# Second experts' rows scattered into token order, with TensorE weighing two of three blocks in the last stage

## The reference, cut to what matters

```python
y = layernorm(x)
topk_vals, topk_idx = top_k(y @ gate_w + gate_b, 2)
topk_w = softmax(topk_vals)
h = relu(y @ w1[e] + b1[e]);  expert_out = h @ w2[e] + b2[e]      # for the two chosen e
z = y + sum_k topk_w[k] * expert_out[topk_idx[k]]
out = x + (z - mean(z)) / sqrt(var(z) + 1e-5) * gamma + beta
```

## Time and profile before

| what | us |
|---|---|
| median of three runs | 5655.62 |
| profiled execution, own time | 5677.49 |
| its span in the trace | 5676.2 |
| experts' loop in its steady part | 5336 to 5586 |
| last stage, from its first instruction | 5594.9 to 5676.2 |

### The profile page before, as it was taken

The page is one execution under the profiler, slowest core; times in us unless marked ns, Lnnn a source line. Parts: engine busy times, 40 slices in busy tenths (PEclk is TensorE's granted clock), DMA queues, the critical chain, the costliest instruction groups (busy, mean ns, idle before and its releaser), DMA issues.

```text
span 5676.2 us, 62271 instructions
## 1 busy us (share of the span) xinstructions
PE 4234.6 (75%) x17066; PEld 2584.4 (46%) x17066; DVE 2738.1 (48%) x6256; ACT 1789.4 (32%) x4055; POOL 2420.1 (43%) x2811
## 2 busy tenths in 40 slices
PE   1111034457999999999999779487777776998798
PEld 0011012223544544545545338376666664665574
DVE  7998012222374254353222222665555557777535
ACT  4333000000100100101000221476666666998221
POOL 3788777774000000000000101677777775887124
PEclk9999567779999999999999889698888998999797
DMA  8900134456332222222322324577778774777423
GB/s 347 373 1 1 35 114 139 139 185 227 102 108 89 99 102 85 106 102 77 120 100 70 119 91 137 166 241 238 244 234 244 236 235 144 241 241 242 161 65 116
DMA packets 382809, 868.12 MB, mean 153 GB/s; under 512 B 87554, under 2 KB 187789, under 8 KB 355218
## 3 DMA queue, kind: packets, MB, share of 16 engines
q1 hardware_dynamic: 252002, 689.14, 34.7%
q0 software_dynamic: 76816, 147.75, 9.9%
q10 hardware_dynamic: 53664, 27.26, 1.7%
HBM read 579.84 MB, written 284.11 MB: 152 GB/s over the span
## 4 chain that ended last, share of the span: by engine, by line
PE 51%; POOL 26%; issue 10%; DVE 7%; DMA 5%; ACT 1%; DVEq 0%; SPq 0%; POOLq 0%; ACTq 0%
PE PS L1118 20%; POOL adjacency_more L581 10%; POOL mem L2043 9%; PE PS L2459 7%; POOL adjacency L581 7%; PE PS L1143 3%; PE PS L1145 3%; DMA mem<-gat_rows,mem 3%; PE PS L2879 2%; PE PS L1691 2%; PE PS L2899 2%; PE PS L1529 2%; PE PS L1148 2%; PE PS L1151 2%; PE PS L2086 1%
## 5 line engine op out<-in xcount | busy, mean ns | idle before, releaser
L1118 PE MATMUL PS<-mem 128*128 128x512 f32 (+1 forms) x3500 | 1400.8, 561 | 465.1 <-DVE mem L1260 461.1
L1118 PEld LDWEIGHTS PS<-mem 128*128 128x128 f32 x3500 | 639.3, 197 | 1187.3 <-issue 709.5
L2043 POOL DMA_INDIRECT mem<-gat_rows,mem x832 | 814.7, 979 | 261.2 <-issue 234.6
L1306 POOL TENSOR_TENSOR mem<-mem 128x256 f32<-128x256 f32 x25 | 20.2, 842 | 1784.1 <-DMA mem<-x 1784.1
L581 POOL DMA_INDIRECT adjacency_more<-mem x526 | 559.2, 1063 | 171.7 <-issue 171.7
L1191 ACT ACTIVATE mem<-PS 128x512 f32<-128x512 f32 (+1 forms) x35 | 19.0, 544 | 1706.8 <-PE PS L1118 1706.8
L2086 PE MATMUL PS<-mem 128*128 128x256 bf16 x2496 | 384.4, 294 | 118.2 <-issue 104.5
L2459 PE MATMUL PS<-mem 128*128 128x264 f32 x1660 | 462.8, 407 | 6.5 <-ACT mem L2447 2.4
L2124 ACT ACTIVATE mem<-PS,mem 128x256 f32<-128x256 f32 x832 | 424.0, 560 | 29.5 <-DVE mem L2151 15.7
L581 POOL DMA_INDIRECT adjacency<-mem x256 | 370.5, 1447 | 96.0 <-issue 80.6
L262 PE MATMUL PS<-mem 106*128 106x106 f32 (+4 forms) x446 | 93.7, 360 | 423.6 <-DVE mem L393 303.5
(11 more groups left out here) (437 smaller groups left out, 6931.1 us busy)
## 6 DMA issues: line engine op xcount, KB each, us to landing
mem<-adjacency SPq DMA_DIRECT2D x150, 1280.0 KB, 5.4
gathered_rows<-mem SPq DMA_DIRECT2D x416, 264.0 KB
mem<-gathered_rows SPq DMA_DIRECT2D x208, 528.0 KB, 4.5
adjacency<-mem SPq DMA_DIRECT2D x56, 800.0 KB, 20.7
adjacency_more<-mem SPq DMA_DIRECT2D x56, 800.0 KB, 21.5
mem<-adjacency_more SPq DMA_DIRECT2D x30, 1280.0 KB, 13.7
adjacency<-mem SPq DMA_DIRECT2D x30, 1280.0 KB, 11.1
mem<-edge_slots ACTq DMA_DIRECT2D x26, 1024.0 KB
```

What stands on the lines that cost most here:

```text
L1118: ins = t.matmul(PS[:, f, 0:n], lhsT=h[:, b, f * 128:(f + 1) * 128], rhs=m.pan[i % NPAN][:, j, 0:n], start=(b == 0), stop=(b == NB - 1))
L2043: g.indirect_dma_start(m.Dg[i % RING][:, k, j, :], None, HD[:, :], bass.IndirectOffsetOnAxis(ap=L.idxD[:, c:c + 1], axis=0)).then_inc(s[f" ...
```

## The change

The tiles' results are no longer stored in the order of the places. Routing also computes, for every place, the row of a new tensor `moe_out` in the tokens' order (first all first choices, then all second choices, in blocks; empty places get spare rows of their own), and GpSimd scatters each tile there by an indirect DMA, six tiles behind its gathers and from three buffers in place of two. The last stage has no gathers: SyncE loads both choices of five blocks at a time plainly, in front of x, and no load waits for anything. In the 16 of 25 blocks whose number is no multiple of three, TensorE forms Y + w1 * first + w2 * second in the other half of the PSUM bank, with the identity and two diagonal matrices that ScalarE makes (32 of them); VectorE reads these blocks' sums from PSUM.

```diff
@@ gates2_vector (tile_b multiplies by block + 1, for the second choice by block + 26)
-    st.mark(v.tensor_copy(m.ft, PS[:, 5, 0:NT1]))
-    v.wait_ge(st.sem, st.n)
-    st.mark(v.scalar_tensor_tensor(m.ft, PS[:, 5, NT1:2 * NT1], 128.0, m.ft, ALU.mult, ALU.add))
+    st.mark(v.tensor_copy(m.to, PS[:, 5, 0:NT1]))
+    st.mark(v.tensor_scalar(m.ft, PS[:, 5, NT1:2 * NT1], float(NB) + 0.5, -128.0 * NB, ALU.is_gt, ALU.mult))
+    v.wait_ge(st.sem, st.n)
+    st.mark(v.scalar_tensor_tensor(m.to, PS[:, 5, NT1:2 * NT1], 128.0, m.to, ALU.mult, ALU.add))
+    v.wait_ge(st.sem, st.n)
+    st.mark(v.scalar_tensor_tensor(m.ft, m.to, -128.0, m.ft, ALU.add, ALU.add))
+    v.wait_ge(st.sem, st.n)
+    st.mark(v.tensor_scalar(m.ft, m.ft, 0.0, None, ALU.max))
     v.wait_ge(st.sem, st.n)
     v.tensor_copy(m.tok, m.ft).then_inc(s["tok"].sem, 1)
...
+    # five more operations of 64 columns, behind tok and eo, that end in m.toi
@@ experts2_gpsimd (SCATTER_LAG = 6, NOG = 3; experts2_sync is gone)
+    def placed(j):
+        g.wait_ge(*gs["to"](1))
+        g.wait_ge(*s["o"](j + 1))
+        g.indirect_dma_start(YO[:, :], bass.IndirectOffsetOnAxis(ap=m.toi[:, j:j + 1], axis=0), m.og[j % NOG],
+                             None).then_inc(s[f"pl{j % NOG}"].sem, 16)
...
+        if i >= SCATTER_LAG:
+            placed(i - SCATTER_LAG)
+    for j in range(NT1 - SCATTER_LAG, NT1):
+        placed(j)
@@ experts2_vector
-            if j >= 2:
-                v.wait_ge(*s[f"st{j % 2}"](16 * (j // 2)))
+            if j >= NOG:
+                v.wait_ge(*s[f"pl{j % NOG}"](16 * (j // NOG)))
@@ finish_sync
+    chosen(0)
     q.dma_start(f.gm, ...); q.dma_start(f.bt, ...)
     kept(0)
-    kept(1)
-    for k in range(2, GRP):
+    for k in range(1, GRP):
+        chosen(k)                       # two loads of 5 x 128 rows of 1 KB
         kept(k)
-        rows(GRP * (k - 2), GRP * (k - 1))
-    for k in range(3, len(ENDS) - 1):
-        rows(ENDS[k - 1], ENDS[k])
+    for k in range(len(ENDS) - 1):
+        rows(ENDS[k - 1] if k else 0, ENDS[k])
@@ finish_tensor (by_array(b) is b % 3 != 0)
-    t.wait_ge(*s["w"](32))
     for b in range(NB):
         if b % GRP == 0:
             t.wait_ge(*s[f"xl{b // GRP}"](16))
         if b >= 8:
             t.wait_ge(*s["rows"](b - 7))
+        if by_array(b):
+            finish_ready(t, s, b)
+            d = array_until(b) - 1
+            t.wait_ge(*s["diag"](2 * d + 2))
+            t.matmul(PS[:, b % 8, 256:512], lhsT=cn.ident, rhs=m.Y[:, b, :], start=True, stop=False)
+            for k in range(2):
+                t.matmul(PS[:, b % 8, 256:512], lhsT=f.dg[0:n, d, k, :], rhs=f.yg[0:n, b, k, :], start=False, stop=(k == 1))
+        if b == 0:
+            t.wait_ge(*s["w"](32))
         t.matmul(PS[:, b % 8, 0:256], lhsT=cn.ident, rhs=f.X[:, b, :], start=True, stop=False)
         t.matmul(PS[:, b % 8, 0:256], lhsT=cn.ones[0:1, :], rhs=f.bt, start=False, stop=True).then_inc(s["kept"].sem, 1)
@@ finish_gpsimd is gone; finish_scalar, ahead of its square roots
+    for b in range(NB):
+        if by_array(b):
+            for k, gate in enumerate((m.wa, m.ew)):
+                c.activation(f.dg[:, array_until(b) - 1, k, :], cn.ident, ACT.Copy, scale=gate[:, b:b + 1])...
@@ finish_vector
+        if by_array(b):
+            v.wait_ge(*s["kept"](b + 1))
+        else:
+            # the two weighted additions into m.Y, as before
-        v.bn_stats(f.st[:, b, :], m.Y[:, b, :])...
+        v.bn_stats(f.st[:, b, :], PS[:, b % 8, 256:512] if by_array(b) else m.Y[:, b, :])...
...
-                v.scalar_tensor_tensor(m.Y[:, c, :], m.Y[:, c, :], f.mv[:, c, 0:1], f.gm, ...)
+                v.scalar_tensor_tensor(m.Y[:, c, :], PS[:, c % 8, 256:512] if by_array(c) else m.Y[:, c, :], f.mv[:, c, 0:1],
+                                       f.gm, ...)
```

More of the change, by code:

```diff
@@ L2489 @@
 NC = 2 * NB
+NOG = 3
+SPARE = NT1 * 128
 def group_of(b):
@@ L2532, in gates_memory @@
     m.eo = ar.mk(2, NT1, dt=I32)
-    m.og = [ar.mk(256) for _ in range(2)]
+    m.og = [ar.mk(256) for _ in range(NOG)]
+    m.toi = ar.mk(NT1, dt=I32)
     route_top = ar.top
@@ L2820, in gates2_vector @@
     v.tensor_copy(m.eo, m.ew4).then_inc(s["eo"].sem, 1)
+    st.mark(v.tensor_scalar(m.pad, cn.pairs[:, 0:NT1], 128.0, cn.pidx, ALU.mult, ALU.add))
+    v.wait_ge(st.sem, st.n)
+    st.mark(v.tensor_scalar(m.pad, m.pad, float(128 - SPARE), None, ALU.add))
+    v.wait_ge(st.sem, st.n)
+    st.mark(v.scalar_tensor_tensor(m.pad, m.to, 0.0, m.pad, ALU.is_equal, ALU.mult))
+    v.wait_ge(st.sem, st.n)
+    st.mark(v.scalar_tensor_tensor(m.to, m.to, float(SPARE - 128), m.pad, ALU.add, ALU.add))
+    v.wait_ge(st.sem, st.n)
+    v.tensor_copy(m.toi, m.to).then_inc(s["to"].sem, 1)
     v.wait_ge(*s["exp"](1))
@@ L2969, in finish_memory, with finish_sync, chosen @@
     return f
[L2972 to L2977, removed]
+FINISH = {"w": 32, **{f"xl{k}": 16 for k in range(GRP)}, **{f"ch{k}": 64 if k == GRP - 1 else 32 for k in range(GRP)}, "diag": 2 * array_until(NB - 1),
+          "taken": 2 * (NB - array_until(NB - 1)), "stats": NB, "mv": NB, "sd": len(ENDS), "rsd": len(ENDS), "kept": NB,
+          "centred": NB, "rows": NB, "out": 96}
+def finish_sync(q, a, m, f, s, XD, YO, out):
     def kept(k):
-        if k:
-            q.wait_ge(*s["taken"](2 * GRP * (k - 1) + 4))
         w = slice(GRP * k * D, GRP * (k + 1) * D)
         q.dma_start(m.W2[:, w], XD[:, w]).then_inc(s[f"xl{k}"].sem, 16)
+    def chosen(k):
+        n = 4 if k == GRP - 1 else GRP
+        for j in range(2):
+            lo = SPARE + j * NB * 128 + GRP * k * 128
+            q.dma_start(f.yg[:, GRP * k:GRP * k + n, j, :],
+                        YO[lo:lo + n * 128, :].rearrange("(b p) d -> p b d", p=128)).then_inc(s[f"ch{k}"].sem, 16)
+        if n == 4:
+            for j in range(2):
+                lo = SPARE + j * NB * 128 + 24 * 128
+                q.dma_start(f.yg[0:TAIL, 24, j, :], YO[lo:lo + TAIL, :]).then_inc(s[f"ch{k}"].sem, 16)
     def rows(lo, hi):
@@ L3001, in finish_sync, with finish_ready, finish_tensor @@
     q.wait_ge(*s["out"](96))
-def finish_tensor(t, f, cn, s, PS):
-    t.wait_ge(*s["w"](32))
+def finish_ready(e, s, b):
+    k = b // GRP
+    e.wait_ge(*s[f"ch{k}"](64 if k == GRP - 1 else 32))
+def finish_tensor(t, m, f, cn, s, PS):
     for b in range(NB):
+        n = rows_of(b)
         if b % GRP == 0:
@@ L3144, in program @@
         YD = dram("moe_in", (NB * 128, D), F32)
-        YSR = dram("moe_out", (NT1 * 128, D), F32)
+        YO = dram("moe_out", (SPARE + NC * 128, D), F32)
         HR = dram("hidden_rows", (NB * 128, 1024), F32)
@@ L3335, in program @@
         experts2_vector(v, m, gs, xs, PS, [v.alloc_register(f"mv{i}") for i in range(8)])
-        join([xs["st0"](512), xs["st1"](512)])
+        join([xs["pl0"](352), xs["pl1"](336), xs["pl2"](336)])
         f = finish_memory(m)
         fs = sg.stage(FINISH, INDIRECT)
-        finish_sync(q, a, m, f, fs, XD, out)
-        finish_gpsimd(g, m, f, fs, YSR)
-        finish_scalar(c, f, fs, cn.epsc)
-        finish_tensor(t, f, cn, fs, PS)
+        finish_sync(q, a, m, f, fs, XD, YO, out)
+        finish_scalar(c, m, f, cn, fs, cn.epsc)
+        finish_tensor(t, m, f, cn, fs, PS)
         finish_vector(v, m, f, fs, PS)
```

65 lines of the change are left out of this document (29 added, 36 removed).

## The result

The changed kernel takes **5672.59 us** (median of 11 runs, 5655.34 to 5685.84) against 5653.09 (5648.39 to 5663.61, 11 runs) before on the same chip: a ratio of 1.0026, 95% interval 1.0015 to 1.0038. Forecast were 5647.4 us and a range of 5638 to 5665. The forecast named the wrong sign, and the result lies outside the range. "Slower" had a chance of 0.16, all of it from rivals (a), (d) and (e), and none of these came.

The account below looks back on a forecast made before the run. TensorE was taken to pace the experts' loop, and a ring of gather, landing and VectorE freeing a buffer the last stage. 67.3 + 0.6 + 1.1 - 77.2 = -8.2 us, from 5655.6 to 5647.4 us; range 5638 to 5665.

Parts of the forecast that it names:

- (a): Rival, last stage: TensorE stays at half clock, so +36.5 us and 5692 us, slower; chance 0.11.
- (d): Rival, last stage: the new matmuls don't hide their weight loads, giving 5706 us; chance 0.02.
- (e): Rival, experts' loop: scatters landing in over 12 us stretch it by 32 us, giving 5680 us; chance 0.03.
- the last line of the sum: Whole kernel: the profile's 21.9 us surplus lies outside what changes, so -8.2 us takes the median to 5647.4.
- Routing +0.6: Before the first gather: two more dependent steps and one independent one add 0.6 us, all on the path.
- Loop 0: Experts' loop: added scatters cost 0 us, covered by TensorE's 4.1 us per tile.
- Join +1.1: Between experts and last stage: waiting for the last scatter to land adds 1.1 us, bounds +0.4 to +1.7.
- TensorE's first block at +8.0: Last stage: loads let TensorE start 8.0 us after the join, bounds 7.5 and 9.7; before it was +5.96.
- Clock: Last stage: TensorE runs blocks 0 and 1 at half clock and rises to full clock after block 1.
- Blocks of 1.15 and 2.45 us at full clock: Last stage, TensorE: a block takes 1.15 us without diagonals and 2.45 with, taking 0.14 per row-count switch.
- Rival (b): Last stage: TensorE holds nobody, switches being free at full clock; end at +60.6, 5640.7 us; chance 0.22.
- Part 6: Last stage, VectorE: alone it would end at +63.9 us; TensorE sets the end, narrowly, at +67.3.

Follow-up runs that it names:

- third group: One chip's comparison of a_again, b_cut, a_vec and the changed kernel without its last stage, beside the kernel before (median 5655.73 us).
- b_same: Kernel before, with only SyncE's ten awaited counts held at 128 or above, as in every follow-up kernel; ratio 0.9990 to the kernel before.
- b_cut_gathers: b_cut with GpSimd's 50 last-stage gathers put back, their rows unused; 6102.45 us, 0.9973 of the kernel before.
- b_big: b_same with its tensor moe_out made 6400 rows of 1 KB larger, the added rows unused; ratio 0.9987 to the kernel before.
- b_cut: b_same without the last stage (rows of Y stored as they are), all adjacency scatters kept; 5621.03 us, 0.9930 of the kernel before.
- a_same: Changed kernel with only SyncE's awaited counts held at 128 or above; ratio 1.0015 to the kernel before.
- a_last: a_same with moe_out allocated last, behind x_kept; ratio 1.0012 to the kernel before.
- a_gathers: a_same with 21 needless gathers from moe_in on GpSimd in the last stage; ratio 1.0000 to the kernel before.
- a_again: The kernel of a_same, unchanged, measured once more on another chip; 5683.50 us against 5655.73 for the kernel before, ratio 1.0046.
- a_vec: a_same with VectorE weighing all 25 last-stage blocks, without diagonals or added matmuls; 5684.42 us.
- a_gaps: a_same with VectorE waiting on itself twice per step of the second half's sort; 5621.20 us, 0.9951 of the kernel before.
- a_gate: a_same with the 782 adjacency scatters begun only after VectorE finished both halves' indices; 6386.42 us, 12.1 us faster than b_gate.
- b_gaps: b_same with VectorE waiting on itself twice per step of the second half's sort; 5618.84 us, 0.9949 of the kernel before.
- b_few: b_same with only 16 of the 256 and 16 of the 526 adjacency scatters; 5263.06 us.
- b_few_cut: b_few without the last stage, rows of Y stored as they are; 5193.54 us.
- b_gate: b_same with the 782 adjacency scatters begun only after VectorE finished both halves' indices; 6398.51 us, 279 above the kernel before.

## Why the prediction was wrong

**The step that failed** is the last line of the sum: that the surplus of the profiled execution "lies outside what changes, so the median goes from 5655.6 to 5647.4". The work ahead of the routing was costed at nothing, with no cover and no bound named. It did change: by the estimates above it grew by 26 us in this comparison, 31 to 34 in the third group and 17 to 22 in the first. The traces hold part of that. Among profiled executions whose longest scatter is 8.0 us, "first" is 426 to 436 us with the 958 ns scatter (b_same, b_cut_gathers and b_big, all on slower chips) and 440 to 447 with 969 (five kernels, on both): some 11 us, more than the gain. On the faster chips before and b_cut, each with a scatter of 37.8 us, differ by 11.7. "Rest" is 727 to 730 against 731 to 736 us on the faster chips: some 4 of the 5.8 that 526 x 0.011 gives, and nothing on the slower ones. Against about 6 us of gain on the faster chips and 9 on the slow, that makes roughly +9 and +2.

Measured were +19.5 and +28 us on faster chips, and +13 (a_same), +8 (a_last) and 0 (a_gathers, with its 21 gathers) on slower ones. The missing 10 to 19 us of the first three are not settled. What could hold them is the long scatter: it puts 11 to 25 us on "first", and it comes in some executions and not in others of one kernel. a_again's profiled execution has none and at 5671.58 is the fastest of its ten, whose others reach 5692.14; a_vec's has one, and at 5685.66 lies at its median. That reads as if most runs of the changed kernel had it. But four of the eleven runs of the main comparison are faster than its profiled one, which has none either; a run without a profile does not show its scatters; and of the profiles with the sort beside and without pauses, a scatter above 10 us stands in two of five with 958 ns and in five of eleven with 969. So the traces give no sign that it is more frequent after the change, and why removing the gathers slows the start stays open.

**The profiled execution itself** was forecast at 5669.3 us and took 5665.28. I had two numbers, 5677.49 and a median 21.9 us lower, and took the difference for spread that needs no cause. Its longest instruction is one scatter of 37.8 us. That 5665.28 came near 5669.3 is luck: about 6 us are the changed part, and the other 6 lie ahead of it, where the long scatter is missing.

**The parts that were forecast** came as follows, against a sum of -8.2 and about -6 measured. Of the 6, 1.9 are no part of the change (see the loop), so it is about -4 against -8.2.
- Routing +0.6: the first gather starts 3.66 us behind the end of the one-hot matmuls, against 3.05. Right.
- Loop 0: 270.3 us before from the first transpose to the last w2 matmul; after 268.4, and 270.2 to 270.3 in a_again, a_gaps and a_gate. Right. The 1.9 us come from TensorE's clock, at full for the second burst of w1 matmuls after (1.98 us) and at half before (3.78). Rival (e) is out: a landing of 2.40 us on the chain.
- Join +1.1: 5585.35 to 5588.53 is 3.18 us, against 1.96, so +1.2. The size was luck. The landing of 2.40 was the shortest that was considered; the issue after `og` took 0.76 us instead of 0.3, and the prediction's lower bound of +0.4 had left it out (2.7 less 1.96 is +0.7).
- TensorE's first block at +8.0, bounds 7.5 and 9.7: measured +10.45, outside. I had counted bytes and latency, not SyncE's time: x's load is issued 2.0 us after the first load, behind two halves of chosen rows, gamma and beta, and lands 8.22 us later, with the next group's loads already in the queue.
- Clock: half for block 0 and most of block 1, full from 5605.3 us on, 0.5 us before block 1 ends, so block 1 took 4.5 us instead of 4.9. Right, but the reason given was thin: a burst of 3.8 us of 128-row matmuls in the experts was followed by half clock in before and by full clock in after. Rivals (a) and (d) are out in the profiled executions.
- Blocks of 1.15 and 2.45 us at full clock: 5608.38 to 5609.63 is 1.25, 5609.63 to 5612.18 is 2.55. A block without diagonals has four records of 0.22, so the two switches between row counts cost 0.38 per block, not 0.28. Rival (b), which had them free, is out. It was also mis-sized: it took 6.7 us off TensorE's +67.3, though Part 6 has VectorE alone at +63.9.
- Statistics from PSUM: 0.43 us, as from SBUF. TensorE sets the end: the chain is TensorE up to 5652.87. VectorE's last row ends at 5659.84, +71.3 after the join instead of +67.3: 2.45 for the start and 22 blocks x 0.1, less 0.4 in block 1 and 0.2 behind block 23.

So the mechanism of the last stage was right, and its size was about half: from the last `og` to the end the span has 78.6 us instead of 83.2, 4.7 less where 8.8 were forecast (5.0 less in a_gaps than in b_gaps, 6.9 in a_same than in b_same, on another chip). The term that missed most is TensorE's start, then the switches. VectorE's own work on the way was 64 us by its terms, not 63, which changed nothing. What a_vec adds: with VectorE weighing all 25 blocks the end part is the same 355.7 us, so the two balance, as Part 6 had them (+63.9 and +67.3).

## What to carry to other kernels

When a profiled execution lies well above its median, find the instruction that holds the surplus before subtracting two numbers; a surplus of 20 us is larger than most changes. Subtracting each kernel's end part from its median shows whether the stages ahead of the change kept their time. Look whether GpSimd issues DMAs beside a VectorE that never pauses: two waits of VectorE on itself per step took 31 to 68 us from the first 256 scatters here and 24 to 27 us from the whole. Judge an edit by the stage it touches and by the total, and where they disagree, leave out stages until the total agrees again.

## What the hardware showed that was not expected

- An indirect DMA's instruction on GpSimd can take 11 ns more or less (958 or 969 ns, of 782) depending on whether 50 gathers from moe_out come 4 ms later in the same program. b_cut and b_cut_gathers differ in nothing else but the chip, and on one chip b_few and b_few_cut differ likewise (958 and 969), which differ in the whole last stage. The cause is open. Going the other way, the 64 gathers from moe_in take 955 ns in b_same and 944 in b_cut.
- One scatter can stand for 6.1, 7.8, 17.4, 29.3 or 37.8 us beside VectorE's sort, though none of VectorE's instructions there takes over 1 us. Its place relative to VectorE's instructions was the same to 0.02 us where it took 7.8 and where it took 37.8.
- The same kernel takes 5646 to 5656 us on some chips and 6119 to 6134 on others. The difference is in the 2400 us stage of the rounds (2650 in b_same) and in the gathers from gat_rows (1070 us and 1284); the second experts take 270.3 us in before and 270.5 in b_gate.
- Matmuls with equal row counts hide their weight loads at either clock; the change from 128 rows to 1 and back costs 0.38 us per block at full clock (1.25 us less four records of 0.22), against 0.56 at half.
